# GpSimd copies the row indices of four expert tiles at once, one group ahead of its gathers

## What is computed

```python
x = x + 0.5 * ffn(layernorm(x)); x = x + attention(layernorm(x)); x = x + 0.5 * ffn(layernorm(x))
def ffn(x):                                   # T = 4096 tokens, D = 256
    weights, indices = top_k(softmax(x @ Wg), 4)   # 4 of E = 32 experts for each token
    for e in range(32):
        tok, w = tokens and weights of the pairs that chose e
        y[tok] += (silu(x[tok] @ W1[e]) * (x[tok] @ W3[e])) @ W2[e] * w      # H = 128
    return y + (silu(x @ Ws1) * (x @ Ws3)) @ Ws2
```

## Time and profile before

| what | us |
|---|---|
| median of three runs | 3503.41 |
| the profiled execution, its own time | 3502.28 |
| its span | 3500.6 |
| TensorE busy in matmuls | 2889.4 |
| ScalarE busy | 2235.2 |
| VectorE busy | 884.2 |
| GpSimd busy | 775.3 |
| gathers of the two expert stages (320), busy on GpSimd | 313.1 |
| idle time of GpSimd before them | 264.8 |

### The profile page before, as it was taken

One profiled execution on the slowest core, in us unless ns is written; L12 is line 12 of the kernel. 1 busy time (PEld: TensorE's weight loads), 2 busy tenths in 40 slices (PEclk: granted clock), 3 DMA queues, 4 the chain that ended last, 5 costly groups with the idle time before them and its releaser, 6 DMA issues. The chain is left out here.

```text
span 3500.6 us, 58137 instructions
## 1 busy us (share of the span) xinstructions
PE 2889.4 (83%) x16837; PEld 1048.6 (30%) x16840; DVE 884.2 (25%) x2256; ACT 2235.2 (64%) x2566; POOL 775.3 (22%) x1140
## 2 busy tenths in 40 slices
PE   4269996566899999999999999999999653999863
PEld 4146663333111111111111111111111251666532
DVE  3753334454000000000000000000000258333253
ACT  1024440033899999999999999999999410344300
POOL 0355556703000000000000000000000205555575
PEclk9999998878999999999999999999999855999986
DMA  5224443334001001001001010010000410344434
GB/s 155 85 81 132 128 131 102 95 116 95 5 4 18 12 7 24 7 4 26 4 14 17 7 23 7 4 25 4 7 4 7 138 60 0 122 132 128 125 96 124
DMA packets 136851, 199.17 MB, mean 57 GB/s; under 512 B 23456, under 2 KB 104352, under 8 KB 135072
## 3 DMA queue, kind: packets, MB, share of 16 engines
q1 hardware_dynamic: 96528, 104.45, 10.9%
q0 software_dynamic: 27648, 75.53, 7.7%
q10 hardware_dynamic: 12496, 16.78, 1.6%
HBM read 120.78 MB, written 75.89 MB: 56 GB/s over the span
## 5 line engine op out<-in xcount | busy, mean ns | idle before, releaser
L1306 ACT ACTIVATE probs<-psS 128x1536 f32<-128x1536 f32 (+1 forms) x1376 | 1851.9, 1451 | 11.5 <-PE psS L1258 6.8
L1278 PE MATMUL psO<-probs,values 128*32 128x512 f32 x8192 | 1096.3, 607 | 0.4 <-ACT probs L1306 0.4
L1258 PE MATMUL psS<-RA 51*128 51x512 f16 x4096 | 824.5, 384 | 116.9 <-ACT probs L1306 88.5
L1258 PEld LDWEIGHTS psS<-RA 51*128 51x128 f16 x4096 | 151.3, 93 | 1146.4 <-ACT probs L1306 1111.1
L1328 DVE COPY sums<-psO 128x512 f32<-128x512 f32 x32 | 22.1, 692 | 1742.2 <-PE psO L1278 1742.2
L1368 POOL TENSOR_TENSOR RA<-RA,pbias 128x1024 f32<-128x1024 f32 x8 | 21.9, 2756 | 1894.1 <-DMA RA<-x_d 1894.1
L545 POOL DMA_INDIRECT xg<-xn_d,index x320 | 313.1, 978 | 264.8 <-PE psX L561 148.2
L569 PE MATMUL psH<-WE,xgt 128*128 x1280 | 357.2, 402 | 0.0
L616 ACT ACTIVATE gate<-psH 128x128 f32<-128x128 f32 x320 | 88.9, 278 | 323.8 <-PE psH L569 323.8
L1278 PEld LDWEIGHTS psO<-probs,values 128*32 128x32 f32 x8192 | 161.7, 108 | 438.0 <-issue 425.4
L678 POOL DMA_INDIRECT Y<-pair_d,cindex x256 | 245.9, 961 | 99.8 <-issue 69.3
(11 more groups left out here) (205 smaller groups left out, 1931.3 us busy)
## 6 DMA issues: line engine op xcount, KB each, us to landing
pair_d<-ob SPq DMA_DIRECT2D x320, 128.0 KB
RA<-part_d SPq DMA_DIRECT2D x96, 128.0 KB
xn_d<-xn SPq DMA_DIRECT2D x64, 128.0 KB, 1.7
part_d<-parts SPq DMA_DIRECT2D x32, 256.0 KB, 2.5
hd<-head_d SPq DMA_DIRECT2D x16, 512.0 KB, 7.0
xg<-xn_d,index POOLq DMA_INDIRECT x320, 2.8
RA<-in_x SPq DMA_DIRECT2D x8, 512.0 KB, 7.8
WE<-in_W ACTq DMA_DIRECT2D x1, 4096.0 KB, 22.9
```

Of the source, the lines that this page charges most:

```text
L1258: last = pe.matmul(psS[m % 2][:, (u - first[m]) * BLK:(u - first[m] + 1) * BLK], K[r][rows, kt * P:(kt + 1) * P], Q[r][rows, at:at + BLK], ...
L1278: last = pe.matmul(psO[q % 2][32 * j:32 * (j + 1), :], values[:, r, j % 2, kt, :], probs[:, m % RING, at:at + BLK], start=(kt == 0), stop= ...
L1306: act.activation(probs[:, m % RING, 0:n], psS[m % 2][:, 0:n], ACT.Exp, scale=SCALE).then_inc(sem("exped"), 1)
```

## The change

Three things change in GpSimd's part of `experts`, and with them the size of two tables.

- The index copy takes four columns at once: one copy for four gathers, 40 a stage and one before the loop, where there were 160.
- The copy of group g + 1 is issued before the gathers of group g, into another of four places of `index`. The wait on `indexed` ahead of the gathers of group g asks for the copy that was issued one group earlier.
- The gather alone waits for `x_turned`. The copy waited for it too before. Each gather keeps its wait on `x_turned` and its increment of `index_seen`.
- The last group copies one group past the end, so `slot_token` gets four more columns, set to zero in `route`.

```diff
-        slot_token = sb(f"slot_token{L}", [P, NJ], I32, keep)
+        slot_token = sb(f"slot_token{L}", [P, NJ + 4], I32, keep)
...
+                pool.memset(slot_token[:, NJ:], 0)
...
-                link(v.tensor_copy(slot_token[:, :], tok_f[:, :]))
+                link(v.tensor_copy(slot_token[:, 0:NJ], tok_f[:, :]))
...
-        index = sb(f"index{L}", [P, U], I32, c)
+        LAPS = 4
+        index = sb(f"index{L}", [P, LAPS, U], I32, c)
...
-                with pool.Fori(0, NJ // U) as i:
-                    for u in range(U):
-                        j = i * U + u
-                        pool.wait_ge(sem("x_turned"), j + 1)
-                        pool.tensor_copy(index[:, u:u + 1], slot_token[:, bass.ds(j, 1)]).then_inc(sem("indexed"), 1)
-                        pool.wait_ge(sem("indexed"), j + 1)
-                        pool.sem_inc(sem("index_seen"), 1)
-                        pool.indirect_dma_start(xg[:, u, :], None, xn_d, bass.IndirectOffsetOnAxis(ap=index[:, u:u + 1], axis=0))\
-                            .then_inc(gathered[u], 16)
+                pool.tensor_copy(index[:, 0, :], slot_token[:, 0:U]).then_inc(sem("indexed"), 1)
+                with pool.Fori(0, NJ // (LAPS * U)) as i:
+                    for w in range(LAPS):
+                        g = i * LAPS + w
+                        pool.tensor_copy(index[:, (w + 1) % LAPS, :], slot_token[:, bass.ds((g + 1) * U, U)])\
+                            .then_inc(sem("indexed"), 1)
+                        pool.wait_ge(sem("indexed"), g + 1)
+                        for u in range(U):
+                            pool.wait_ge(sem("x_turned"), g * U + (u + 1))
+                            carried(pool, sem("index_seen"))
+                            pool.indirect_dma_start(xg[:, u, :], None, xn_d,
+                                                    bass.IndirectOffsetOnAxis(ap=index[:, w, u:u + 1], axis=0))\
+                                .then_inc(gathered[u], 16)
```

## The result

The changed kernel took 3408.84 us, the median of four runs (3406.18 to 3411.32); the kernel before took 3503.21 us beside it (four runs, 3502.83 to 3503.52). The ratio is 0.9727, 95% interval 0.9714 to 0.9739: 2.7% faster. The forecast was 3435 us in a range from 3405 to 3462. The direction and the range held, the range by only 4 us; the gain was 94 us where 68 were forecast.

What follows compares the result with a forecast made beforehand. GpSimd's gathers, one every 1.98 us, were taken to bound both expert stages. With TensorE next at 1.7875 us a tile, 70.6 us saved less 1.5 us a stage left 67.6 us: 3435 us, range 3405 to 3462.

Steps and rivals of the forecast that it cites:

- What bounded the kernel: In both expert stages GpSimd sets the pace, one gather every 1.98 us, and is never held back by TensorE.
- the rival in which the pause stays: On GpSimd, 0.81 us precedes any gather with a wait and increment: 1.84 us a tile, 3457 us; chance 0.12.
- What GpSimd costs afterwards: In the expert stages, four gathers with one copy cost GpSimd 5.89 us, 1.47 us a tile, or 1.33 with 0.30.
- my bounds: On GpSimd, the pause between a copy made ahead and the next gather: from 0.30 to 0.88 us, 0.88 taken.
- Coming in time: Gathers land 3.7 us after tile j - 4 is turned; TensorE wants them at 6.8 us, so 3.1 us spare.
- TensorE's pace: In the expert stages TensorE binds next: four steps in 7.15 us, 1.7875 us a tile, for the whole stage.
- the prediction's own sign: Wrong on TensorE if four turns took under 6.9 or over 7.3 us with no wait for a DMA.
- the first rival: In the expert stages TensorE runs faster, 6.87 us for four steps, 1.72 a tile: 3413 us; chance 0.12.
- The 1.5 us that I gave back for the start: At each expert stage's start, about one step of extra time not due to gathers; estimated between 0 and two steps.
- The register load: On TensorE's sequencer, one load in every step: 0.30 us median, 0.60 longest, already contained in the 1.79 us a tile.
- the slower rival: Longer register loads on TensorE's sequencer, 0.60 us each, make a step 2.09 us: 3528 us; chance 0.03.
- the rival of slow gathers: In the expert stages landing grows past 5.9 us and binds; at 6.5 us, 1.94 a tile, 3483 us; chance 0.08.

## Why the prediction was right, and where it was off

**What bounded the kernel** was right. GpSimd set the pace, at one gather in 1.98 us, and the whole gain came out of the two stages in which it did. The reading of the 0.81 us as one fixed cost, the wait for the copy's own semaphore, is shown by the copies one tile ahead, which leave 0.16 of it, together with the four not ahead, which keep 0.89. That rules out the rival in which the pause stays. The 0.03 us above 1.98 had one more cause than I named: the slow landings of the last tiles, about 1.1 us of the 4.5 to 4.9 a stage.

**What GpSimd costs afterwards** was right in what counts. The 0.30 us from the combine stage is what the changed kernel shows. The pause behind a copy made ahead is 0.16 us, below both ends of my bounds, which took it for at least that behind a gather. It didn't move the sum, as stated. One figure beside the sum was wrong: 0.19 us in four tiles would be 15 us in both stages, 8 in one.

**Coming in time** was right up to the last tiles of each stage. Gathers are issued about 5.4 us before their turn where 2.8 are needed. The long pause of 3.5 us is still there and cost TensorE 0.33 us of idle time where it had cost 3.19.

**TensorE's pace** is the term that was mis-sized: 1.7875 us a tile where 1.685 was measured, 159 x 0.1025 = 16.3 us a stage, 33 us in all. By the prediction's own sign, four turns in under 6.9 us with no wait for a DMA, it was wrong on TensorE: they took 6.76. The step that failed is the sentence that after the late gather "seven turns begin with no wait for a DMA between them" and so show TensorE's own pace. They do show no wait, and yet they waited. I had not laid beside them when each of those gathers landed, which the same trace tells. The gathers issued at 365.54, 367.52 and 369.51 us, one by one:

```profile
L545 POOL DMA_INDIRECT xg<-xn_d,index x1: 977/977/977, 365.5 to 365.5; - x1
...
DMA to landing us min/median/max: 3.1/3.1/3.1
```

```profile
L545 POOL DMA_INDIRECT xg<-xn_d,index x1: 977/977/977, 367.5 to 367.5; - x1
...
DMA to landing us min/median/max: 3.0/3.0/3.0
```

```profile
L545 POOL DMA_INDIRECT xg<-xn_d,index x1: 977/977/977, 369.5 to 369.5; - x1
...
DMA to landing us min/median/max: 2.8/2.8/2.8
```

They landed at 368.7, 370.5 and 372.3, and the next one, issued at 371.50, at 374.3. The turns of the earlier trace rows begin at 368.75, 370.54, 372.52 and 374.30. Up to 368.75 TensorE was making good its delay, at 1.71 and 1.63 us a step; from there on it had caught up with the gathers, and its steps were theirs again. The profile names a wait only where the engine stood idle, and here TensorE still had the last tile's matmuls in hand when its sequencer began to wait. The sequencer's own rows show it. Behind the turn's weight load, in the order of the code, stands register work (L564; L570 in the changed kernel). Here it is for the turn at 368.75, and in the changed kernel for the turn at 241.89:

```profile
L564 PEldq FUSED_REGOPS  x1: 41/41/41, 368.7 to 368.7; - x1
```

```profile
L570 PEldq FUSED_REGOPS  x1: 41/41/41, 241.6 to 241.6; - x1
```

In the changed kernel the sequencer is some 0.3 us ahead of the array. In the kernel before it got past the wait only as the gather landed, at 368.7, and for the next turn at 370.5; it had no lead left. What that costs shows inside the step, under another name:

```profile
370.21 0.30 PEld L584 LDWEIGHTS psO<-WE,hidt 128*128 128x128 f32 x2 [0.22 <-issue]
```

These weight loads come 1.46 us after their turn's, where it is 1.30 in a step of 1.63 us (368.42 after 367.12), and the next turn stands directly behind them. It is so throughout: inside the loops of the first stage (tiles 10 to 143) they come 1.38 us after their turn's at the median where the sequencer has no lead (50 turns) and 1.30 us where it has (16). The kernel with two tiles ahead shows such a step again, in a stage where gathers bind; the kernel with three ahead shows that a short lead by itself doesn't make it. The 1.98 us at the loop's end went the same way: 1.77 in the changed kernel.

So the first rival, a faster TensorE, is what happened. I gave it 0.12 and put it at 3413 us, for the reason that 1.63 us comes only once in four steps of the earlier trace rows. In the changed kernel it comes twice in four, and the step at the loop's end is 1.77 and not 1.98.

That the time still fell into the range is partly luck. The lower bound of 3405 us was set for that rival, and with the pace alone corrected the forecast would have been some 3402 us, outside the range. The slow end of the stage, which was no part of the forecast, put some 7 us back: 3435 - 33 + 7 = 3409.

**The end of the stage** was no term of the forecast, and it cost the other way. It stood in the trace of the kernel before: the longest landing, 4.1 us, for which the prediction found room, is one of these tiles, whose median there is 3.9. The tiles that hold no pair take about 2 us a step, 2.2 us more in the first stage and 5.1 in the second than at 1.685. By the measured terms the first stage is 159 x 1.685 = 267.9, 0.5 for the start (the first eight steps take 13.96 us, not 13.5), 2.2 for the end and 0.3 for the long pause: 270.9 us, measured 271.1. The 1.5 us that I gave back for the start were too many by one in the first stage and by half a microsecond in the second, whose first eight steps take 14.5 us.

**The register load.** The Trainium skill's floor of about 600 ns (DMA: Bandwidth & Descriptors, Latency and other measured facts) would have kept a step at 2.09 us. In the changed kernel the load has

```profile
L579 PEldq TENSOR_LOAD <-tile_expert x320: 296/307/557, 204.4 to 3204.8; - x160
```

a median of 0.307 us and steps of 1.63 us with one such load each. The trace disagrees with the page, and the slower rival falls with it. The gathers' landing stayed at a median of 2.8 us at 150 GB/s, so the rival of slow gathers falls too, but for the tail: there landing passed the 5.9 us that it named, and the gathers bound again.

## What to carry to other kernels

A wait for one's own last instruction costs 0.8 us every time here, from GpSimd's copy to its gather; issue the instruction one round earlier, or one for several rounds, and either is enough once the engine is below the pace of the next one. Before a stretch without recorded waits is taken for an engine's own pace, lay the arrival of its inputs beside its starts: a wait that begins while the engine still has work in hand leaves no idle time at that instruction, and what it costs can stand at a later one as "issue". And give empty work different addresses, or leave it out.

## What the runs showed of the hardware

- An indirect DMA of 128 rows of 1 KB lands in 2.8 us when the rows differ. With one row read 128 times it took 3.9 us with the gathers 1.98 us apart (the kernel before), and 6.3 us where gathers were issued four tiles ahead, with the DMA engines 95% busy at 130 GB/s; with 128 different rows for the same tiles 47% at 150 GB/s, and the last turns came every 1.63 us.
- GpSimd can start a gather 0.16 us after a copy that it doesn't wait for, less than the 0.30 us between two gathers, and 0.81 to 0.89 us after one that it waits for.
- On TensorE's sequencer the branch at the end of a loop takes 0.21 us. In a loop of four tiles it left the array idle for 0.18 us.
- Once a stage, in every kernel here, GpSimd paused 3.1 to 3.6 us ahead of one gather, the 114th. Its cause stays open; with gathers four tiles ahead all but 0.33 us of it is hidden.
